# Flamingo block on one core: the attention slot's transposes in one block, its output products in one block, and where in PSUM they land

## What is computed

```
x = x + tanh(g_xattn) * attention(layernorm(x), ctx)     # 16 heads of 32, softmax over 77 keys
x = x + tanh(g_ffn)   * ffn(layernorm(x))                # 512 -> 1408 (gate, up) -> 512
# ffn: activations and weights rounded to 8-bit steps, silu(gate) * up between
```

## Time and profile before

| | |
|---|---|
| median of 3 runs | 638.42 us (637.68 to 639.74) |
| profiled execution | 636.91 us, span 635.1 us |
| PE busy | 613.6 us, 97% of the span |
| PEld busy | 461.9 us, 73% |
| DVE busy | 510.3 us, 80% |
| ACT busy | 352.1 us, 55% |
| POOL busy | 197.1 us, 31% |

### The profile page before, as it was taken

One profiled execution on the slowest core, in us unless ns is written; L12 is line 12 of the kernel. 1 busy time (PEld: TensorE's weight loads), 2 busy tenths in 40 slices (PEclk: granted clock), 3 DMA queues, 4 the chain that ended last, 5 costly groups with the idle time before them and its releaser, 6 DMA issues. The chain is left out here.

```text
span 635.1 us, 12602 instructions
## 1 busy us (share of the span) xinstructions
PE 613.6 (97%) x3841; PEld 461.9 (73%) x3862; DVE 510.3 (80%) x954; ACT 352.1 (55%) x512; POOL 197.1 (31%) x416
## 2 busy tenths in 40 slices
PE   8999999999999999999999986999999999899997
PEld 6699999999999999999999864444444444444544
DVE  6688788888988888899988657788888888866764
ACT  4264567566566656656664343555555554365553
POOL 7112333333333333323421202111111110057775
PEclk9999999999999999999999998999999999999999
DMA  8748422222222223312411000286446110099623
GB/s 305 207 115 249 121 59 68 58 66 47 58 60 58 66 58 68 78 36 77 97 42 50 25 0 1 48 239 221 132 137 211 26 29 12 0 341 418 266 109 123
DMA packets 85206, 69.61 MB, mean 110 GB/s; under 512 B 64915, under 2 KB 67373, under 8 KB 85165
## 3 DMA queue, kind: packets, MB, share of 16 engines
q1 hardware_dynamic: 79377, 52.13, 29.6%
q10 hardware_dynamic: 5788, 16.98, 7.4%
HBM read 32.48 MB, written 21.36 MB: 85 GB/s over the span
## 5 line engine op out<-in xcount | busy, mean ns | idle before, releaser
L1343 ACT ACTIVATE sb_silu<-ps_g,sb_sgu 128x512 f32<-128x512 f32 x88 | 60.5, 687 | 72.1 <-PE ps_g L1430 42.8
L1430 PE MATMUL ps_g<-sb_xqT,sb_wgu 128*128 128x512 bf16 x344 | 89.3, 379 | 1.0 <-DVE sb_xqT L1386 0.6
L1430 PE MATMUL ps_u<-sb_xqT,sb_wgu 128*128 128x512 bf16 x346 | 89.4, 379 | 0.3
L603 ACT COPY sb_pT<-ps_p 128x512 f32<-128x512 f32 (+1 forms) x96 | 46.4, 521 | 69.6 <-PE ps_p L1042 69.6
L1053 PE MATMUL ps_o<-sb_vblk,sb_pT 128*128 (+4 forms) x640 | 79.1, 270 | 3.3 <-ACT sb_pT L603 2.5
L1401 DVE SCALAR_TENSOR_TENSOR sb_h<-ps_u,sb_sgu,sb_silu 128x512 f32<-128x512 f32 (+1 forms) x88 | 66.1, 751 | 19.8 <-PE ps_u L1430 19.4
L1053 PEld LDWEIGHTS ps_o<-sb_vblk,sb_pT 128*128 128x128 f32 (+1 forms) x640 | 76.9, 191 | 4.7 <-ACT sb_pT L603 3.5
L986 PE MATMUL ps_q<-sb_xT_hi,sb_wq_hi 128*128 128x256 f32 x256 | 77.9, 304 | 0.0
L988 PE MATMUL ps_q<-sb_xT_hi,sb_wq_lo 128*128 128x256 f32 x256 | 72.3, 282 | 0.0
L987 PE MATMUL ps_q<-sb_xT_lo,sb_wq_hi 128*128 128x256 f32 x256 | 72.2, 282 | 0.0
L1636 PE MATMUL ps_z<-sb_wdT,sb_hq 128*128 128x512 bf16 x324 | 71.4, 379 | 0.3
(11 more groups left out here) (227 smaller groups left out, 1331.0 us busy)
## 6 DMA issues: line engine op xcount, KB each, us to landing
h_spill<-sb_h SPq DMA_DIRECT2D x4, 2816.0 KB, 8.8
sb_h<-h_spill ACTq DMA_DIRECT2D x16, 704.0 KB, 7.1
out_dram<-sb_wgu SPq DMA_DIRECT2D x31, 256.0 KB, 2.0
sb_x<-in_x_dram ACTq DMA_DIRECT2D x1, 4096.0 KB, 18.3
sb_w_in<-in_L_ffn_w_gate_dram SPq DMA_DIRECT2D x11, 256.0 KB, 2.6
sb_w_in<-in_L_ffn_w_up_dram SPq DMA_DIRECT2D x11, 256.0 KB, 2.6
sb_x<-in_x_dram SPq DMA_DIRECT2D x2, 1024.0 KB, 14.9
sb_x<-in_x_dram SPq DMA_DIRECT2D x2, 512.0 KB, 5.0
```

Source lines behind the costliest of these rows:

```text
L1343: act.activation(silu[(j * KI + i) % 2][:, :, :].rearrange("p t n -> p (t n)"), p_g[(j * KI + i) % 2][:, :], ACT.Silu, scale=sgu[:, i:i + ...
L1430: last = pe.matmul(banks[(j * KI + i) % 2][:, :], wgu[:, what, k, i * P:(i + 1) * P], xqT[j][:, k, :], start=(k == 0), stop=(k == KD - 1))
```

## The change

The third chunk of the transposes goes to a bank of its own, `p_c2`, which lies in the bank that held the outputs. The outputs of half 0 go to the bank of chunk 0 (`p_p[0]`) and those of half 1 to the bank of chunk 1 (`p_p[1]`). All three chunks are transposed in one block ahead of the first queries; both halves of the outputs are computed in one block behind the second scores and ahead of the second queries. The semaphore waits move with the banks. ScalarE copies all three chunks before it computes L598. On VectorE the second maximum comes ahead of the first reciprocal, the second reciprocal ahead of the second subtraction, the second normalisation behind that subtraction, and `x_part` ahead of `stats_end`. In slot 1 the first queries come ahead of the transposes. A second memset clears the rows of `p_c2` that the 104-row piece leaves.

```diff
@@ -173,7 +173,10 @@
                 p_x = pb("x", [P, KD, P])
                 p_p = [pb(f"p{i}", [P, 4, P]) for i in range(2)]
                 p_ob = pb("o", [P, 512])
-                p_o = p_ob[:, 0:HH * VW].rearrange("p (h d) -> p h d", h=HH)
+                p_c2 = p_ob[:, 0:2 * P].rearrange("p (k n) -> p k n", k=2)
+                p_o = [a[:, :, :].rearrange("p k n -> p (k n)")[:, 0:HH * VW].rearrange("p (h d) -> p h d", h=HH)
+                       for a in p_p]
+                p_pT = [p_p[0], p_p[1], p_c2]
                 p_y = pb("y", [P, D])
 
 
@@ -587,20 +590,20 @@
                             act.copy(oT(n - 2)[0], p_x[:, :, :]).then_inc(a_ohi, 1)
                         if isinstance(n, int) and n == 1:
                             act.wait_ge(l_v[0], 16 * SLOT0[KB])
-                        for c, (k0, k1) in enumerate(CHUNKS):
-                            if c == 2 and runs(n - 4, NT - 1):
-                                wait(act, g_nb2, n - 3)
-                                wait(act, v_xmax, n - 3)
-                                if isinstance(n, int) and n >= PLANES_FREE:
-                                    act.wait_ge(v_xlo, NT)
-                                else:
-                                    wait(act, v_x1, n - 2)
-                                act.activation(xabs(n - 4), row(n - 4), ACT.Abs, bias=nb2[:, span(n - 4)],
-                                               scale=rs2[:, span(n - 4)]).then_inc(a_abs, 1)
-                            if runs(n - 1, NT):
+                        if runs(n - 1, NT):
+                            for c, (k0, k1) in enumerate(CHUNKS):
                                 wait(act, t_p, 3 * (n - 1) + c + 1)
                                 wait(act, t_o, 2 * (n - 1) - (c == 0))
-                                act.copy(pT[:, k0:k1, :], p_p[c % 2][:, 0:k1 - k0, :]).then_inc(a_p, 1)
+                                act.copy(pT[:, k0:k1, :], p_pT[c][:, 0:k1 - k0, :]).then_inc(a_p, 1)
+                        if runs(n - 4, NT - 1):
+                            wait(act, g_nb2, n - 3)
+                            wait(act, v_xmax, n - 3)
+                            if isinstance(n, int) and n >= PLANES_FREE:
+                                act.wait_ge(v_xlo, NT)
+                            else:
+                                wait(act, v_x1, n - 2)
+                            act.activation(xabs(n - 4), row(n - 4), ACT.Abs, bias=nb2[:, span(n - 4)],
+                                           scale=rs2[:, span(n - 4)]).then_inc(a_abs, 1)
                         for half in range(2):
                             if runs(n, NT):
                                 wait(act, v_sub, 2 * n + half + 1)
@@ -727,13 +730,13 @@
                     def outputs_rec(n, half):
                         wait(dve, t_o, 2 * n + half + 1)
                         wait(dve, v_o, 2 * n + half)
-                        dve.reciprocal(rden[:, half, :], p_o[:, :, HD]).then_inc(v_rec, 1)
+                        dve.reciprocal(rden[:, half, :], p_o[half][:, :, HD]).then_inc(v_rec, 1)
 
                     def outputs_norm(n, half):
                         wait(dve, v_rec, 2 * n + half + 1)
                         wait(dve, t_oT, n)
                         dve.tensor_tensor(o_sb[:, half * HH * HD:(half + 1) * HH * HD]
-                                          .rearrange("p (h d) -> p h d", h=HH), p_o[:, :, 0:HD],
+                                          .rearrange("p (h d) -> p h d", h=HH), p_o[half][:, :, 0:HD],
                                           rden[:, half, :].unsqueeze(2).broadcast_to([P, HH, HD]), ALU.mult)\
                            .then_inc(v_o, 1)
 
@@ -857,6 +860,8 @@
                         down_part(n, 0)
                         if runs(m, NT):
                             dve.bn_aggr(mvt[:, :], bn2[:, 0, :]).then_inc(v_st2, 1)
+                        if runs(n, NT):
+                            scores_max(n, 1)
                         if runs(n - 1, NT):
                             outputs_rec(n - 1, 0)
                         if runs(n, NW):
@@ -865,8 +870,6 @@
                             dve.reciprocal(w_inv[:, :], w_am[:, :]).then_inc(v_winv, 1)
                         if runs(n - 1, NT):
                             outputs_norm(n - 1, 0)
-                        if runs(n, NT):
-                            scores_max(n, 1)
                         if runs(n, NW):
                             wait(dve, v_winv, n + 1)
                             wait(dve, g_wbf, n)
@@ -876,12 +879,17 @@
                         if runs(n - 4, NT):
                             wait(dve, a_abs, n - 3)
                             dve.tensor_reduce(xmax[:, span(n - 4)], xabs(n - 4), X, ALU.max).then_inc(v_xmax, 1)
+                        if runs(n - 1, NT):
+                            outputs_rec(n - 1, 1)
                         if runs(n, NT):
                             scores_sub(n, t, 1)
+                        if runs(n - 1, NT):
+                            outputs_norm(n - 1, 1)
                         if isinstance(n, int) and n == 0:
                             values(1)
                             dve.wait_ge(v_v, 2 * B)
                             dve.memset(p_p[1][:, 0, :], 0.0).then_inc(v_zero, 1)
+                            dve.memset(p_c2[:, 1, :], 0.0).then_inc(v_zero, 1)
                             dve.tensor_scalar(sg_1[:, :], sg_e[:, :], 1.0, None, ALU.add).then_inc(v_sig, 1)
                             dve.wait_ge(v_sig, 1)
                             dve.reciprocal(sig[:, :], sg_1[:, :]).then_inc(v_sig, 1)
@@ -897,19 +905,15 @@
                                 dve.wait_ge(l_x[4], 16)
                             if isinstance(n, int) and n + 6 == NT - KD:
                                 dve.wait_ge(l_x[5], 16)
-                        if runs(n - 1, NT):
-                            outputs_rec(n - 1, 1)
                         if runs(n + 6, NT):
                             stats(n + 6)
                         if runs(n + 6, NT):
                             wait(dve, v_bn, n + 7)
                             wait(dve, g_nb, n + 5)
-                        if runs(n - 1, NT):
-                            outputs_norm(n - 1, 1)
+                        if runs(n + 4, NT):
+                            x_part(n + 4, t)
                         if runs(n + 6, NT):
                             stats_end(n + 6, t)
-                        if runs(n + 4, NT):
-                            x_part(n + 4, t)
 
                     dve.sem_inc(v_xmax, 1)
                     dve.wait_ge(g_id, 1)
@@ -1033,25 +1037,27 @@
 
                     def prob_transpose(n, t, c):
                         wait(pe, a_exp, 2 * n + (1 if c == 0 else 2))
-                        wait(pe, a_p, 3 * n + (0, -1, 1)[c])
+                        if c < 2:
+                            wait(pe, v_o, 2 * n - 1 + c)
+                        else:
+                            wait(pe, a_p, 3 * n)
                         if isinstance(n, int) and n == 0:
-                            pe.wait_ge(v_zero, 1)
+                            pe.wait_ge(v_zero, 2)
                         k0, k1 = CHUNKS[c]
                         for k in range(k0, k1):
                             half, j = divmod(k, KB)
-                            last = pe.transpose(p_p[c % 2][0:ROWS[j], k - k0, :],
+                            last = pe.transpose(p_pT[c][0:ROWS[j], k - k0, :],
                                                 prob[t % 2][:, half, P * j:P * j + ROWS[j]], identf[:, :])
                         last.then_inc(t_p, 1)
 
                     def outputs(n, half):
                         wait(pe, a_p, 3 * n + 2 + half)
-                        wait(pe, v_o, 2 * n + half)
                         b = n // (S // P)
                         for j in range(KB):
                             first, end = heads_of(j)
                             rows = slice(0, ROWS[j])
                             last = pe.matmul(
-                                p_o[:, first:end + 1, :].rearrange("p h d -> p (h d)"),
+                                p_o[half][:, first:end + 1, :].rearrange("p h d -> p (h d)"),
                                 pT[rows, half * KB + j, :],
                                 vblk[rows, span(b), half, SLOT0[j]:SLOT0[j + 1], :]
                                 .rearrange("p a s d -> p (a s d)"),
@@ -1113,25 +1119,25 @@
                             return
                         if runs(n, NT):
                             scores(n, t, 0)
+                        opening = isinstance(n, int) and n == 1
+                        if opening:
+                            queries(n + 2, (t + 2) % 4, 0)
                         if runs(n - 2, NT - 1):
                             out_transpose(n - 2)
                         if runs(n - 1, NT):
-                            prob_transpose(n - 1, (t - 1) % 4, 0)
```

(12 more changed lines are left out.)

## The result

The changed kernel took 639.5 us (median of 20 executions, 638.05 to 642.9), the kernel before 637.43 us (median of 20, 636.23 to 641.02). The ratio is 1.0025, with a 95% interval of 1.0014 to 1.0037: slower by about 1.6 us (the two medians by themselves lie 2.1 apart). That is inside the 0.3% that the forecast called no change, though the interval reaches beyond it, and inside the range. That the range held it was in part luck. Of the four terms of the sum two came in as forecast, the gain at the end was 0.3 us larger, and the loop was off by 1.9 us with the slots behind it. And the forecast started from 638.42, the median of three executions; over twenty the kernel before has 637.43, so 639.5 lies only 1.0 above the forecast 638.5 but 2.1 above the kernel before.

The account below looks back on a forecast made before the run. TensorE's gapless list of work was taken to bound the middle of attention; 0 + 0.7 + 1.2 - 1.9 = 0.0 us of change, so from the median of 638.42 it predicted 638.5 us, range 636.7 to 640.9.

Parts of the forecast that it names:

- TensorE's list, nothing: Attention, TensorE's own work: joining the blocks of outputs changes no counts and saves 0 us.
- late first step: Rival, faster: one late step of 0.08 us per slot at a border of outputs is saved, 636.2 us; chance 0.10.
- a closer stream in longer blocks: Rival, faster: 30 pairs per slot each go 0.03 us faster, 25 us over 28 slots, 613 us; chance 0.02.
- The second queries end one block later and start a chain: Middle slots: L580 starts 1.12 us later, delaying L694, L716 and L722; second scores stall 0.09 us in eight loop slots.
- the prediction's own sign of failure: Prediction fails if loop slots take 11.25 us or more, all slots fall under 11.05, or the start loses 3 us.
- L694 0.65 later: Chain step in the loop: VectorE's L694 starts 0.65 us after ScalarE's L575.
- the slower rival: Loop chain closes later than summed, through register waits or TensorE's wait; 0.15 longer gives 3.6 us, 641.4; chance 0.18.
- Start, +1.2: Slots 1 and 2: late second queries delay L694, TensorE's wait for it grows by 1.37 us; +1.2 us in all.
- End, -1.9: Slots 30 onward: -0.66 in slot 30, +0.23 in slot 31, -0.55 and -0.92 in the last slot; -1.9 us.
- The sum: Whole kernel: 0 + 0.7 + 1.2 - 1.9 = 0.0 us.
- the loop's term: Loop slots: eight stalls of 0.09 us as TensorE's second scores wait for L722; +0.7 us.

Follow-up runs that it names:

- the places alone: Kernel before with the new places in PSUM and the waits that belong to them, every engine's order as before: 636.16 us, ratio 0.9965.

## Why the prediction was right and wrong, step by step

- **TensorE's list, nothing.** Right. Without stalls the loop takes 177.62, against 177.68 before. Neither the late first step nor a closer stream in longer blocks exists: those rivals fall.
- **The second queries end one block later and start a chain.** Right in every step but one, and in the place where it closes: 8.65 us into the slot for `q_hi`, and it is the second scores that wait. But the prediction's own sign of failure, loop slots of 11.25 us or more, came true: the 16 take 11.26 on average, and 11.22 to 11.34 behind the first.
- **"L694 0.65 later".** This is the step that failed, though the sum stayed in its range. It was measured in the kernel before, where the instruction had two waits, and was carried over to one with four. The prediction's argument against the slower rival, that all other steps are measured in the loop, was true of the durations and not of this wait. With 0.17 more there, and the 0.05 less that L725 took, the stalls would be 0.21 and 0.12 us in turn: 2.6 in 16 slots, less 0.11 in each of the four that have 0.71, so 2.2. Measured: 2.40 in the loop, and 0.22 in the written-out slots behind it, against 0.7 and 0.
- **The slower rival.** It named the right chain, the right sign and the size within a factor (3.6 for the loop and the slots behind it, against 2.62), but put the missing time into registers and TensorE's wait in the loop. The runs put it elsewhere: TensorE's wait took 0.24, and the written-out slots have the 0.82 as well. The page that it named, Advanced Engine Details and Errata of the Trainium skill, section on network and comms, gives 50 to 100 ns for reading a semaphore from a sequencer. The extra 0.06 to 0.20 us of these runs do not speak against it.
- **Another page would have helped.** In the Trainium skill, Perfetto Trace Analysis says in its section on DVE / Act engine instructions that such an instruction is decoded and then pushed into a wait queue, where it waits for its semaphores while the sequencer is ready for the next one. Its section on sequencer-only instructions has these wait in the sequencer, which takes up the next one only afterwards. The trace agrees: with the late wait on `x_part` itself it begins 0.03 us after L578's end, with the late wait ahead of it 0.09 to 0.23 after.
- **Start, +1.2.** Right: +1.26, and 1.27 come back when slots 1 and 2 are undone.
- **End, -1.9.** Right in sign and place: -0.64 in slot 30 (forecast -0.66), -1.56 behind it (forecast -1.24). The undersized term is the last slot's, 1.73 instead of 1.47: with the places alone the projection behind the third chunk starts 0.76 us sooner in the slot, where 0.55 was taken. The new order of VectorE in slot 31 costs 0.17 instead of 0.23, and only 0.06 of it comes with the second reciprocal, which the prediction named; 0.11 are there without it.
- **The sum.** +1.74 in attention where 0.0 stood; the measured ratio of 1.0025 is 1.6 us. That this counts as no change is owed to the width of 0.3%, and to the end's extra 0.3 us, and not to the loop's term, of which the forecast had about a quarter. The 0.06 of slot 3 and how the 0.22 spread over slots 20 to 29 I have not taken apart.

## What to carry to other kernels

When an instruction is moved in front of a neighbour, look at the waits between the two: it inherits them, and an instruction whose late wait is no longer carried by itself started 0.06 to 0.20 us later here. That costs nothing while the engine has slack and its full price in every round once the chain closes. And a busy share of 100% with an empty list of waits does not mean that there are no stalls: the changed kernel's loop shows 180.08 us busy of 180.08 and lost 2.4 of them, which the start to start times show. Last, before a median is set against a sum of stretches, look at the granted clock of the executions behind it.

## What the runs showed of the hardware

- The time from a ScalarE instruction's start to that of the VectorE instruction that waits for it was 0.65 us with the late wait on the instruction itself, 0.71 with it in a semaphore instruction right ahead, 0.82 with it alone in one and one more such instruction between, and 0.85 with it in a pair and a further pair between. The ScalarE instruction lasts 0.62 in all four cases.
- After a wait of 2.07 us for the keys (TensorE busy for 1.93 us of the stretch from 22 to 26), the granted clock fell to 0.50, the 1.2 GHz level, from 28 to 29.5 us, and was 1.00 again from 31 us on; the scores in between came every 0.26 us instead of 0.14. In the nine other traces this wait took 0.39 to 1.60 us and the clock stayed at 1.00.
- The kernel before took 637.0 us on average in 13 executions with a mean granted clock of 0.996 or more, and 638.8 us in 13 with 0.991 or 0.992. A stage that no edit touched took 77.96 to 78.53 us where the clock stayed at 1.00 at its start, and 79.30 to 79.52 where it fell (0.53 from 554 to 556 us in the changed kernel).
